# Attention products made in pairs, a step later, with four steps of probabilities kept

## What is computed

```python
scores = jnp.einsum('bhqd,bhkd->bhqk', q, k) / math.sqrt(hd)
causal = jnp.tril(jnp.ones((l, l), bool))
scores = jnp.where(causal, scores, -jnp.inf)
att = jax.nn.softmax(scores, axis=-1)
out = jnp.einsum('bhqk,bhkd->bhqd', att, v)
```

## Time and profile before

| | us |
|---|---|
| median of three launches | 624.41 |
| lowest, highest | 623.15, 629.63 |
| the profiled launch | 620.05 |
| its span, first to last instruction | 618.3 |
| mean granted TensorE clock | 0.994 of full |

### The profile page before, as it was taken

The page is one execution under the profiler, slowest core; times in us unless marked ns, Lnnn a source line. Parts: engine busy times, 40 slices in busy tenths (PEclk is TensorE's granted clock), DMA queues, the critical chain, the costliest instruction groups (busy, mean ns, idle before and its releaser), DMA issues.

```text
span 618.3 us, 9492 instructions
## 1 busy us (share of the span) xinstructions
PE 597.6 (97%) x3758; PEld 398.9 (65%) x3758; DVE 373.7 (60%) x554; ACT 293.2 (47%) x513; POOL 77.1 (12%) x106
## 2 busy tenths in 40 slices
PE   7899999999999999999999999899999999999996
PEld 6688888877888887777677765444444444444444
DVE  5776645137644324885755446668898888871225
ACT  3655424124523222522212114777787677776772
POOL 3000000000000000502311112121112112121210
PEclk9999999999999999999999999899999999999999
DMA  5614242211120112377914743261616340101003
GB/s 174 203 69 136 69 130 74 102 35 65 39 69 34 52 51 64 89 191 213 170 58 139 138 137 69 49 114 29 120 44 103 78 65 27 24 17 31 16 12 137
DMA packets 24068, 53.14 MB, mean 86 GB/s; under 512 B 8384, under 2 KB 8896, under 8 KB 24016
## 3 DMA queue, kind: packets, MB, share of 16 engines
q1 hardware_dynamic: 23736, 51.96, 32.6%
q0 software_dynamic: 288, 0.58, 0.3%
HBM read 39.63 MB, written 10.60 MB: 81 GB/s over the span
## 4 chain that ended last, share of the span: by engine, by line
PE 83%; DVE 8%; ACT 6%; DMA 2%; issue 2%; SPq 0%; DVEq 0%; ACTq 0%
PE bank L1332 12%; PE bank L1315 10%; PE slot L1012 9%; PE bank L1012 9%; PE slot L1014 8%; PE slot L1013 8%; PE bank L1014 8%; PE bank L1013 8%; PE slot L1226 6%; ACT probs L995 4%; PE slot L1234 2%; DMA x_sb<-in_x 1%; PE slot L1315 1%; DMA stage<-in_stream 1%; DVE maxcol L1685 1%
## 5 line engine op out<-in xcount | busy, mean ns | idle before, releaser
L995 ACT ACTIVATE probs<-bank 128x512 f32<-128x512 f32 (+2 forms) x294 | 144.3, 567 | 47.6 <-PE bank L1315 44.1
L1685 DVE TENSOR_REDUCE maxcol<-slot 128x2 f32<-128x1024 f32 (+2 forms) x112 | 124.9, 1142 | 29.7 <-PE slot L1226 15.0
L1012 PE MATMUL slot<-xt_hi,ring_hi 128*128 128x512 f32 (+3 forms) x248 | 96.4, 389 | 4.0 <-DVE h_lo L1585 1.8
L1014 PE MATMUL slot<-xt_hi,ring_lo 128*128 128x512 f32 (+3 forms) x248 | 95.9, 387 | 0.0
L1013 PE MATMUL slot<-xt_lo,ring_hi 128*128 128x512 f32 (+3 forms) x248 | 95.8, 386 | 0.0
L1332 PE MATMUL bank<-probs,v_sb 128*32 128x512 f32 (+3 forms) x768 | 83.2, 507 | 0.1
L1315 PE MATMUL bank<-qst,kst 50*128 50x512 f32 (+3 forms) x275 | 72.7, 422 | 6.0 <-ACT probs L995 4.2
L1315 PEld LDWEIGHTS bank<-qst,kst 50*128 50x128 f32 x275 | 32.8, 188 | 60.5 <-ACT probs L995 56.0
L787 POOL TENSOR_SCALAR_AFFINE_SELECT probs<-probs 128x512 f32<-128x512 f32 x64 | 41.7, 651 | 181.3 <-ACT probs L995 181.3
L1685 DVE TENSOR_REDUCE maxrest<-slot 128x2 f32<-128x768 f32 (+3 forms) x48 | 49.9, 1046 | 19.7 <-PE slot L1234 19.5
L1226 PE MATMUL slot<-kst,qst 48*128 48x512 f32 (+3 forms) x288 | 56.8, 388 | 0.3 <-DVE maxcol L1685 0.3
(11 more groups left out here) (221 smaller groups left out, 862.9 us busy)
## 6 DMA issues: line engine op xcount, KB each, us to landing
stage<-in_stream SPq DMA_DIRECT2D x43, 512.0 KB, 3.5
qst<-heads_dram SPq DMA_DIRECT2D x12, 256.0 KB, 5.1
kst<-heads_dram SPq DMA_DIRECT2D x12, 256.0 KB, 7.7
heads_dram<-attn_hi SPq DMA_DIRECT2D x4, 512.0 KB
heads_dram<-attn_lo SPq DMA_DIRECT2D x4, 512.0 KB
out_y<-x_sb SPq DMA_DIRECT2D x8, 256.0 KB, 2.1
stage<-u_sb SPq DMA_DIRECT2D x56, 32.0 KB, 2.0
stage<-den_dram SPq DMA_DIRECT2D x14, 128.0 KB
```

The lines of the kernel that those rows point to most:

```text
L995: act.activation(probs[:, to:to + heads, 0:n], score_ps(b)[:, 0:heads * n].rearrange("p (h n) -> p h n", n=n), ACT.Exp, scale=HD ** -0.5). ...
L1012: pe.matmul(out_ap, a[0], b[0], start=start, stop=False)
L1014: return pe.matmul(out_ap, a[1], b[0], start=False, stop=stop)
L1685: dve.tensor_reduce(per_head[:, :, slots[0]:slots[-1] + 1], scores, AX.X, ALU.max).then_inc(S["max_free"], 1)
```

## The change

The products no longer stand behind the scores of every step. Up to step (6, 3) they stand behind the scores of every odd step, for two steps together: those of `i - 3` and then those of `i - 2`. From (6, 4) on (`SINGLE_FROM` is 76) they stand one by one as before. So the products of an even step come one step later, and those of an odd step stand where they stood.

Since the products of step `i - 3` may still be to come when the exponentials of step `i` run, SBUF now holds the probabilities of four steps (`PROB_STEPS`). The fourth step's place is a tensor of its own, `probs_more`, in the memory of `hw1`, which is done with by then. The first exponential of step `i` waits for the products of step `i - 4`. `take_u` stands behind the step in which the last products of a half were made; for each half that is the same step as before.

```diff
-NPROB = GH * (LAG + 1)
+PROB_STEPS = 4
...
+SINGLE_FROM = STEPS * (GROUPS - 2) + MAX_END + 1
+
+
+def weighed_after(i):
+
+    if i >= SINGLE_FROM:
+        return [i - LAG]
+    return [i - 3, i - 2] if i % 2 and i > 1 else []
+
+
+def taken_before(g, half):
+
+    last = STEPS * g + (HT, STEPS)[half] - 1
+    return 1 + next(i for i in range(STEPS * GROUPS) if last in weighed_after(i))
...
+        def probs_of(k):
+
+            r = k % PROB_STEPS
+            return probs_more[:, :, :] if r == PROB_STEPS - 1 else probs[:, GH * r:GH * (r + 1), :]
...
-                    if s == HT + LAG:
+                    if STEPS * g + s == taken_before(g, 0):
                         take_u(g, 0)
-                    if s == LAG and g > 0:
+                    if g > 0 and STEPS * g + s == taken_before(g - 1, 1):
                         take_u(g - 1, 1)
                     n, heads = step_width(s), per_bank(s)
-                    if STEPS * g + s > LAG:
-                        act.wait_ge(S["pv_done"], STEPS * g + s - LAG)
+                    if STEPS * g + s >= PROB_STEPS:
+                        act.wait_ge(S["pv_done"], STEPS * g + s - PROB_STEPS + 1)
...
-                        k = STEPS * g + s - LAG
-                        if hh == GH - 1 and k >= 0:
-                            weigh_values(k)
+                        if hh == GH - 1:
+                            for k in weighed_after(STEPS * g + s):
+                                weigh_values(k)
```

More of the change, by code:

```diff
@@ L404, in build @@
         v_sb = sb(block1, "v_sb", [P, NT, HEADS // 2, 3 * HD])
-        probs = sb(block1, "probs", [P, NPROB, HALF])
+        probs = sb(block1, "probs", [P, GH * (PROB_STEPS - 1), HALF])
         u_sb = sb(block1, "u_sb", [P, 2, HALF])
-        hw1 = [sb(block1, f"hw1_{n}", [P, TOK], F32R) for n in ("hi", "lo")]
+        lora1 = ExitStack()
+        with lora1:
+            hw1 = [sb(lora1, f"hw1_{n}", [P, TOK], F32R) for n in ("hi", "lo")]
+        probs_more = sb(block1, "probs_more", [P, GH, HALF])
         den = sb(block1, "den", [P, 2, DEN_COLS])
@@ L783, in _ @@
                     if s in DIAGONAL:
-                        b = GH * (STEPS * g + s) % NPROB
                         pool.wait_ge(S["exp_done"], banks_before(g, s + 1))
-                        part = probs[:, b:b + GH, 0:P]
+                        part = probs_of(STEPS * g + s)[:, :, 0:P]
                         pool.affine_select(out=part, in_=part, compare_op=ALU.is_ge, fill=0.0, base=0,
@@ L992, in _ @@
                         hh = HEAD_ORDER[place] if heads == 1 else heads * place
-                        to = (GH * (STEPS * g + s) + hh) % NPROB
                         act.wait_ge(S["st_ready"], b + 1)
-                        act.activation(probs[:, to:to + heads, 0:n],
+                        act.activation(probs_of(STEPS * g + s)[:, hh:hh + heads, 0:n],
                                        score_ps(b)[:, 0:heads * n].rearrange("p (h n) -> p h n", n=n),
@@ L1332, in weigh_values @@
                     last = pe.matmul(bank[3][32 * hh:32 * hh + 2 * HD, c0:HALF], v_sb[:, j, (GH * g + hh) // 2, HD * (hh % 2):HD * (hh % 2 + 2)],
-                                     probs[:, (GH * k + hh) % NPROB, 0:HALF - c0], start=(j == 0), stop=stop)
+                                     probs_of(k)[:, hh, 0:HALF - c0], start=(j == 0), stop=stop)
                 last.then_inc(S["pv_done"], 1)
```

## The result

| | before | changed |
|---|---|---|
| median of four launches, us | 623.78 | 644.41 |
| lowest, highest | 620.31, 629.63 | 640.68, 647.61 |
| profiled launch, us | 620.05 | 641.4 |
| its span | 618.3 | 639.7 |
| its mean granted clock | 0.994 | 0.969 |

The change makes the kernel slower: 1.0343 times the time before (95% interval 1.0289 to 1.0396), about 20.6 us. The sign is as forecast, the time is 9 us above the forecast and 0.4 us outside the range.

The account below looks back on a forecast made before the run. PE was taken to be gated by ACT and DVE through the score ring and maxima slots. Windows +7.2 us and clock +3.6 us gave +10.8, so 635.2 us against the median of 624.41; range 622 to 644.

Parts of the forecast that it names:

- What bounds the kernel: Groups 1 to 5: PE's busy time includes waits; ACT and DVE gate it through three score banks, 49.7 us on exponentials.
- What the change saves: Boundaries between scores and products: 37 go at 0.35 us each, 13 us at most if PE never waited.
- The six windows: Two-step stretches of each group, from even step's first score to the next's: 1.3 us longer a group, +7.2 us altogether.
- the walk: Step-by-step timing of PE, ACT and DVE through each two-step window, trusted to 1 or 2 us in the whole.
- The clock: TensorE's falls to half clock after waiting stretches: three more at 1.2 us each, +3.6 us.
- Rival 4: Clock falls once or twice in every group, ten more: +7.2 + 12 = 19 us, 643.6 us; chance 0.11.
- Signals: Gated windows 0.3 to 0.6 us longer, pairs 0.88 apart, score weight-load waits above 49.7 us, over two half-clock stretches.

Follow-up runs that it names:

- e5_short_before: Kernel before, with exponentials of all groups and reductions of maxima from group 2 on working on a quarter of their columns; 607.21 us.
- e6_short_after: Changed kernel, with exponentials of all groups and reductions of maxima from group 2 on working on a quarter of their columns; 608.99 us.
- e3_join_free: Changed kernel with products joined only in the windows of steps 0-1, 6-7 and 8-9; 629.83 us, ratio 1.01 to before.
- e2_filled: Changed kernel with 17 matmuls of zeros added in each of groups 0 to 5 where PE waits; 629.83 us, 1.0102 of before.
- e1_four_kept: Changed kernel with four steps of probabilities kept but no step's products joined; 632.39 us against 626.10 before.
- e8_third: Kernel before, with products in steps 0, 6 and 11 placed behind the third score, not the fourth; 612.04 us, ratio 0.9813.
- e4_join_gated: Changed kernel with products joined only in the windows of steps 2-3, 4-5 and 10-11; 645.92 us, ratio 1.0252 to before.

## Why the prediction was right and wrong

- **What bounds the kernel: right.** The gates of ACT and DVE set the windows. With their work cut to a quarter, the six windows of group 1 take 25.04 us in place of 27.81 (e5_short_before).
- **What the change saves: right in kind.** The six joins of a group paid 0.9 us together where little gated (e6_short_after). Priced at 0.35 each, they would have paid 2.1, so the 13 us were twice too high even as a bound. In the timeline the second products of a pair begin 0.88 us behind the first (e.g. 527.56 and 528.44), without a gap, as predicted. The Trainium skill ("TensorEngine Tiling (Array Packing)", Key Properties) names the drain between modes; the runs agree that a boundary costs something, about 0.16 us on average (0.94 over six) and not the 0.35 I gave it. What of it is drain and what the weight load behind it no run shows, nor the 0.10 that I put for the way into the products.
- **The six windows: right.** Five of them within 0.12 us of the walk, 1.26 us a group for 1.3; 7.4 us at full clock for +7.2. For steps 0 and 1 other kernels show it: 5.32 where e3_join_free has no fall, and 5.32 and 5.75 in e2_filled, so the join is worth nothing there, as walked. The layout costs nothing (e1_four_kept).
- **The clock: this step failed.** It said three more falls at 1.2 us, 3.6 us. The profile has eight more stretches of 3.4 us in the attention, and one ahead of it. The six from 446.8 on cost 1.24 to 1.65 us each against the same windows at full clock (6.97 and 5.32, 7.37 and 5.75), 1.5 on average: most of them begin after short waits and then hit the joined products, not a waiting PE. Over launches, of the 20.6 us between the medians 7.4 are windows, so the term is about **13 us and not 3.6**. It is mis-sized in count, eight or nine falls for three, and in price, 1.5 for 1.2. I had placed three between none and ten "since the short waits of groups 1 to 5 brought only one" fall: that counted one launch of before, which was one of its best (0.994; the mean of 51 is 0.980, some seven stretches). Here a kernel that was near a fall in each group came to one in each of groups 1 to 5 when work was taken from the stretches where PE waits. Rival 4, at 0.11, had the mechanism, and its 643.6 us is within 1 us; that close it is luck, since nine falls at 1.5 cost about what its ten at 1.2 do.
- The page "TensorE: Matmul & The Clock Gate" of the Trainium skill, A second HAM failure mode: psum-queue depth-cycling, gave the direction. The trace agrees with it: in 437 to 574 us, with six falls, no recorded gap of PE was longer than 0.59 us, and PE was busy for 128.2 of 137.0 us.
- **Signals.** Windows, joined starts and the number of half-clock stretches came as said. One did not: the scores' weight loads were to wait longer for exponentials than the 49.7 us of the earlier trace rows. In 437 to 574 us, nearly as long a stretch of the same groups, they waited less:

```profile
ACT probs L1017 <- PE bank L1337: 27.3, 26, 2.7
...
PEld bank L1337 <- ACT probs L1017: 19.1, 66, 0.7
...
PEld bank L1337 <- issue: 12.3, 18, 1.7
```

Here 5.6 us more are put down to `probs_more`. The sum of waits on weight loads is no measure of a gate: it also falls in e2_filled (11.7) at nearly the same windows. Why was not settled.

What stays open: why the clock falls in steps 0 and 1 in particular, and why the gated joins alone lose as much as all six. How few matmuls of zeros would do, and at which places, is not known. Whether e8_third lost its falls to its fuller windows or to another distribution of work was not tried apart.

## What to carry to other kernels

Before moving matmuls out of a stretch where TensorE waits, ask what is left to keep its clock up there: work in a wait is not free to move, and here the loss came later, in the joined products. Judge a kernel's distance from a fall by the mean granted clock of many launches, not by one profile. When PE waits for a ring, moving the independent work a little earlier into the wait (behind the third score and not the fourth) gave 13.5 us, while joining it, which saves drains, cost 20.6.

## What the runs showed of the hardware

- One kernel, unchanged, took 617.8 to 636.9 us, and the time goes with the mean granted clock (0.96 to 0.997, correlation 0.987), at 4.8 us for 0.01.
- A single stretch at half clock was mostly 3.4 us long, but 30.7 us in one launch of e1_four_kept and 20.5 in one of e4_join_gated.
- Matmuls of zeros on `bank[3]`, 102 in all, at places where PE waited, made the changed kernel 14.6 us faster.
- Two steps' products in a row did not bring the clock down where the other engines' work was short: no fall from group 1 up to the last microseconds in the profile of e6_short_after.
